# The fp8 product and the eight-head attention of a gated block, joined into one unrolled pipeline by batch

## The reference, cut to what matters

```python
def fake_quant_fp8(t):
    amax = jnp.max(jnp.abs(t))
    scale = FP8_E4M3_MAX / jnp.maximum(amax, 1e-12)
    q = (t * scale).astype(jnp.float8_e4m3fn).astype(jnp.float32)
    return q / scale
# L2_ffn
xq, wq = fake_quant_fp8(x), fake_quant_fp8(weight)
return jnp.einsum('bsd,od->bso', xq, wq) + bias
# L3_xattn: HEADS = 8, DIM_HEAD = 64, SCALE = 64 ** -0.5
q = (x @ Wq).reshape(B, Nq, HEADS, DIM_HEAD)
k = (context @ Wk).reshape(B, context.shape[1], HEADS, DIM_HEAD)
v = (context @ Wv).reshape(B, context.shape[1], HEADS, DIM_HEAD)
sim = jnp.einsum('bihd,bjhd->bhij', q, k) * SCALE
attn = jax.nn.softmax(sim, axis=-1)
out = jnp.einsum('bhij,bjhd->bihd', attn, v)
out = out.reshape(B, Nq, HEADS * DIM_HEAD)
return out @ Wo + bo
# how they are joined
x = x + jnp.tanh(g_ffn[2]) * L2_ffn(layernorm(x))
x = x + jnp.tanh(g_xattn[3]) * L3_xattn(layernorm(x), ctx)
```

## Time and profile before

| | before |
|---|---|
| median of 3 runs | 1619.43 us |
| profiled execution: its time, its span | 1622.06 us, 1620.3 us |
| busy share of the span | PE 75%, DVE 63%, ACT 42%, POOL 34% |
| `fp8_product`, first to last DVE instruction | 993.6 to 1028.8 us |
| `stage_attention8`: start, first scores, last addition to x | 1029.1, 1053.3, 1330.0 us |
| `stage_moe`, first instruction | 1330.7 us |

### The profile page before, as it was taken

One profiled execution on the slowest core, in us unless ns is written; L12 is line 12 of the kernel. 1 busy time (PEld: TensorE's weight loads), 2 busy tenths in 40 slices (PEclk: granted clock), 3 DMA queues, 4 the chain that ended last, 5 costly groups with the idle time before them and its releaser, 6 DMA issues. The chain is left out here.

```text
span 1620.3 us, 31081 instructions
## 1 busy us (share of the span) xinstructions
PE 1211.6 (75%) x10597; PEld 822.1 (51%) x10597; DVE 1017.7 (63%) x3901; ACT 688.1 (42%) x1990; POOL 548.5 (34%) x758
## 2 busy tenths in 40 slices
PE   2277664666677678965989882578888879999997
PEld 2154222343344446643777771255556556777765
DVE  6346759999991498633677776664645554534442
ACT  2133335665664344311445441164646453433342
POOL 5978876887864365313232310000000000000000
PEclk9569875757667799975999996689999898898988
DMA  6400040000003211000000000000000000000001
GB/s 150 126 2 2 1 116 8 20 24 17 28 20 108 71 37 34 14 14 7 2 3 3 3 3 0 11 1 10 0 10 10 1 1 1 1 0 0 0 0 52
DMA packets 64560, 36.94 MB, mean 23 GB/s; under 512 B 24053, under 2 KB 61553, under 8 KB 64435
## 3 DMA queue, kind: packets, MB, share of 16 engines
q1 hardware_dynamic: 63130, 35.02, 7.9%
q10 hardware_dynamic: 1304, 0.33, 0.1%
HBM read 25.21 MB, written 6.42 MB: 20 GB/s over the span
## 5 line engine op out<-in xcount | busy, mean ns | idle before, releaser
L2693 DVE SCALAR_TENSOR_TENSOR k_X<-ps,m_gt,k_X 128x128 f32 (+1 forms) x256 | 72.1, 344 | 126.0 <-PE ps L2592 126.0
L2622 ACT ACTIVATE m_hid<-ps,k_b 128x512 f32<-128x512 f32 x128 | 81.8, 684 | 138.1 <-PE ps L2592 127.7
L2592 PEld LDWEIGHTS ps<-k_w,m_hid 128*128 128x128 f32 x1024 | 123.1, 192 | 26.8 <-issue 17.2
L2583 PE MATMUL ps<-m_xnT,k_w 128*128 128x512 f32 x256 | 131.1, 644 | 1.1 <-DVE m_lg L2638 1.1
L2592 PE MATMUL ps<-k_w,m_hid 128*128 128x128 f32 x1024 | 123.4, 275 | 0.0
L2476 ACT ACTIVATE l_p<-ps,l_shift 128x128 f32<-128x128 f32 x256 | 89.9, 377 | 73.9 <-DVE l_shift L2521 73.9
L2114 DVE TENSOR_REDUCE g_top<-ps 128x8 f32<-128x1024 f32 x64 | 75.4, 1219 | 50.7 <-PE ps L1982 50.7
L121 POOL TENSOR_TENSOR m_rstd<-m_ve,k_half 128x8 f32<-128x8 f32 x4 | 6.5, 1636 | 286.3 <-DVE m_ve L114 286.3
L1379 DVE MATCH_REPLACE8 c_left<-c_top,c_left 128x128 f32<-128x128 f32 x384 | 100.9, 275 | 0.0
L2062 ACT ACTIVATE g_pT<-ps 128x1024 f32<-128x1024 f32 x64 | 62.1, 1022 | 84.9 <-PE ps L1998 84.9
L121 POOL TENSOR_TENSOR l_rstd<-l_ve,k_half 128x8 f32<-128x8 f32 x4 | 6.5, 1636 | 234.6 <-DVE l_ve L114 234.6
(11 more groups left out here) (523 smaller groups left out, 3275.7 us busy)
## 6 DMA issues: line engine op xcount, KB each, us to landing
v_toep<-kpad SPq DMA_DIRECT2D x4, 1024.0 KB, 10.6
fo_dram<-c_fo SPq DMA_DIRECT2D x32, 128.0 KB, 1.7
v_late<-kpad SPq DMA_DIRECT2D x4, 1024.0 KB, 10.5
d_fo<-fo_dram SPq DMA_DIRECT2D x8, 512.0 KB, 3.6
k_X<-in_x SPq DMA_DIRECT2D x8, 256.0 KB, 3.6
out<-k_X SPq DMA_DIRECT2D x4, 512.0 KB, 5.3
f_cx<-in_ctx SPq DMA_DIRECT2D x4, 384.0 KB, 4.9
c_cx<-in_ctx SPq DMA_DIRECT2D x4, 384.0 KB, 3.5
```

Of the source, the lines that this page charges most:

```text
L2583: pe.matmul(ps[:, 4 * u + q, :], k.w1_3[:, e, 128 * q:128 * q + 128], xnT[:, u], start=True, stop=True).then_inc(s["hid_ps"].sem, 1)
L2592: m = pe.matmul(ps[:, 4 * u + 2 + e % 2, j * S:j * S + S], hid[:, u, q, j * S:j * S + S], k.w2_3[:, e, q, :], start=q == 0, stop=q == 1)
L2622: act.activation(hid[:, u, q, :], ps[:, 4 * u + q, :], ACT.Gelu, bias=k.b1_3[:, 2 * e + q:2 * e + q + 1]).then_inc(s["hid"].sem, 1)
L2693: dve.scalar_tensor_tensor(out=xj[u][j], in0=ps[:, 4 * u + 2 + e % 2, j * S:j * S + S], scalar=gt[:, u, j, e:e + 1], in1=xj[u][j], op0=ALU ...
```

## The change: what it does, and the diff

`fp8_product` and `stage_attention8` become one function, `fp8_attention8`, with one block and no loops: 49 steps, n = -15 to 33, written out on every engine. Step n works at several batches and groups at once:

- scores, maxima, exponentials and values of batch n+1; transposes of the weights, the copies of them and weights times values of batch n; output projection and addition to x of batch n-1.
- `item(n)`: for group (n+5)//4, one quarter (128 of 512 columns of the weight) of the keys' and of the queries' projection. Both go through PSUM bank 6, one after the other.
- once in four steps, `due(n, lead)`: the parts of the fp8 product and of the norm of a group, 15 to 6 steps ahead of the group's first batch: bias added to x on POOL (15), scaling on ACT (14), rounding on DVE (13), transpose (12), product (11), addition to x and statistics (10), power on POOL (9), normalising on DVE (7), transpose, copy and the attention's bias on POOL (6).
- The shares move from DVE (one instruction for eight heads) to POOL (two instructions of four heads).
- The copy of the attention result moves from ACT to DVE, the scaling of x for fp8 from DVE to ACT, both bias additions from DVE to POOL.
- The statistics are closed by `bn_aggr` in place of seven small instructions.
- Keys and values are projected from `k.cT` directly; the DMA to `ct` is gone.
- Exponentials are issued in two halves, with the copies of the transposed weights between them.

The diff, cut to the calls and to one part for each engine:

```diff
-        fp8_product(nc, w, ps, k)
+        fp8_attention8(nc, w, ps, k)
...
-        stages = [stage_front, stage_film, stage_mix, stage_attention16, stage_fp8,
-                  stage_attention8, stage_moe]
+        stages = [stage_front, stage_film, stage_mix, stage_attention16, stage_fp8, stage_moe]
...
-                    sp.dma_start(ct[:, u], k.cT[:, bass.ds(t * 2 * W + u * W, W)]).then_inc(s[f"ct{u}"].sem, 16)
...
+                    pe.wait_ge(q_done, 4 * g + b)
+                    pe.wait_ge(xnT_done, begun(n - 1, 6))
+                    pe.wait_ge(xqT_done, begun(n - 1, 12))
+                    pe.matmul(ps[:, 6, :], k.wk3[:, 128 * b:128 * b + 128], k.cT[:, W * g:W * g + W], start=True,
+                              stop=True).then_inc(k_ps, 1)
+                if 0 <= n - 1 < B:
+
+                    i = n - 1
+                    pe.wait_ge(oT_done, i + 1)
+                    pe.wait_ge(v_done, min(i + 2, B))
+                    pe.wait_ge(x8_done, begun(n - 1, 11))
...
-                        dve.tensor_tensor(p[:, a], p[:, a], total[:, a, :].rearrange("p (h o) -> p h o", o=1)
-                                          .broadcast_to([128, H, 128]), ALU.mult).then_inc(s["share"].sem, 1)
...
-                        act.activation(oT[:].rearrange("p a b -> p (a b)"), ps[:, 6, :],
-                                       ACT.Identity).then_inc(s["oT"].sem, 1)
...
+                if 0 <= n + 1 < B:
+                    i = n + 1
+                    dve.wait_ge(p_done, H * (i + 1))
+                    if i >= 3:
+                        dve.wait_ge(share_done, 2 * (i - 2))
+                    dve.reciprocal(rsum[:, i % 3, :], total[:, i % 3, :]).then_inc(rsum_done, 1)
+                if 0 <= n < B:
+                    dve.wait_ge(av_ps, n + 1)
+                    if n >= 2:
+                        dve.wait_ge(out_ps, n - 1)
+                    dve.tensor_copy(oT[:, n % 2].rearrange("p a b -> p (a b)"), ps[:, 4, :]).then_inc(oT_done, 1)
```

More of the change, by code:

```diff
@@ L2240, in _ @@
             dve.tensor_copy(k.wqT[:], ps[:, 2, 0:64].bitcast(BF16))
[L2243 to L2314, removed]
@@ L2337, in stage_attention8 @@
+        top, shift = tmp("top", [128, 2, H]), tmp("shift", [128, 2, H])
+        total, rsum = tmp("total", [128, 3, H]), tmp("rsum", [128, 3, H])
+        p, pT = tmp("p", [128, 3, H, 128]), tmp("pT", [128, 2, H, 128])
+        oT = tmp("oT", [128, 2, 4, 128])
         bo = tmp("bo", [128, 128])
[L2338 to L2340 removed]
@@ L2341, in stage_attention8 @@
         once = ctx.enter_context(OneTime(nc, "l_"))
-        bo_done = once("bo")
-        block = ctx.enter_context(nc.Block())
-        @block.sync
-        def _(sp):
-            with sp.Fori(0, TURNS) as t:
-                for u in range(2):
-                    s["v_ps"].wait(sp, t, 0)
-                    sp.dma_start(ct[:, u], k.cT[:, bass.ds(t * 2 * W + u * W, W)]).then_inc(s[f"ct{u}"].sem, 16)
+        q8_done, exponent, magic, sum_done, xq_done, xqT_ps, xqT_done, o8_ps, xb8_done, x8_done = (
+            once(n) for n in ("q8_done", "exponent", "magic", "sum_done", "xq_done", "xqT_ps", "xqT_done", "o8_ps",
+                              "xb8_done", "x8_done"))
@@ new lines, in fp8_attention8, with due, begun, item @@
+        block = ctx.enter_context(nc.Block())
+        FIRST, LAST = -15, B + 2
+        def due(n, lead):
+            g = (n + lead) // G
+            return g if (n + lead) % G == 0 and 0 <= g < GROUPS else None
+        def begun(n, lead):
+            return min(max((n + lead) // G + 1, 0), GROUPS)
+        def item(n):
+            g, b = (n + 5) // G, (n + 5) % G
+            return (g, b) if 0 <= g < GROUPS else (None, b)
+        def group(g):
+            return k.X[:, G * g:G * g + G, :]
@@ L2357, in _ @@
         @block.tensor
         def _(pe):
-            def opening(t, part):
-                if part == 0:
-                    s["p"].wait(pe, t, 0)
-                    s["ct0"].wait(pe, t, 16)
-                    for b in range(4):
-                        pe.matmul(ps[:, b, :], k.wk3[:, 128 * b:128 * b + 128], ct[:, 0], start=True,
-                                  stop=True).then_inc(s["k_ps"].sem, 1)
-                else:
-                    s["pT"].wait(pe, t, 0)
-                    for u in range(2):
-                        transpose_tokens(pe, s, t, u, xn, ps[:, 4 + u, :], k.ident[:])
@@ L2450, in _, with weights @@
         @block.scalar
         def _(act):
[L2452 removed]
+            def weights(i, a):
                 for b in range(4):
[L2454 to L2485 removed]
```

369 lines of the change are left out of this document (207 added, 162 removed).

## The result

The changed kernel took 1569.57 us (median of 4 runs, 1564.09 to 1571.86) beside 1620.12 us for the kernel before (4 runs, 1618.54 to 1624.72): ratio 0.9679, 95% interval 0.9645 to 0.9712. Forecast were 1567.4 us and 1550 to 1590. The profiled execution took 1568.18 us, its span is 1566.2, against 1620.3 before.

The account below looks back on a forecast made before the run. DVE bounded the old fp8 product and a chain the attention; PE would bound new plain steps. Steps 224.4, fill 36.5, steps -1 and 0 14, drain 7.5: 282.4 against 336.5 us, gain taken as 52, so 1567.4, range 1550 to 1590.

Parts of the forecast that it names:

- Part 1: Plain pipeline step: PE's work sums to 6.92 us, against ACT 4.6 and DVE 4.1, so PE bounds it.
- Part 2: Chain within a step, scores to weights times values: 6.26 us, fits into 6.92 with 0.66 spare; shares on POOL hidden.
- Part 3: Steps with group work, by n mod 4: 9.2, 7.0, 7.5 and 7.2 us; projection's wait for the product's addition 1.75.
- Part 4: DVE beside POOL: shift held by POOL's bias addition at n mod 4 = 1, 0.6 us added per four steps.
- Rival B: Pipeline steps: every shift held about 1 us by POOL's shares, 26 steps about 0.8 longer, 1588 us; chance 0.25.
- Part 5: Fill and drain: first scores at 1030 at the low clock, steps -1 and 0 take 14 us, drain 7.5.
- The sum: Rewritten stretch: 282.4 us against 336.5, a gain of 54, taken as 52 for small semaphore waits.
- Rival A: Faster: clock rises in the fill, step -1 already fast, wait for the product's addition costs nothing; 1549 us, chance 0.17.
- C: Rival, slower: waits on banks 6 and 7 drop PE's clock to 0.50; 12 cold steps give 1650 us; chance 0.02.
- D: Rival: fp8 work stays exposed on in-order queues, giving the product's 35 us back; 1602 us, chance 0.03.

Follow-up runs that it names:

- shares_dve: The changed kernel with its shares on VectorE (DVE) again, as two multiplies right behind the reciprocal, POOL without them: 1603.2 us.
- bias_late: The changed kernel with POOL's two bias additions of a group waiting until the shift of their step is done: 1563.27 us.
- x8_first: The changed kernel with DVE's addition of the fp8 product to x moved ahead of the maximum of its step: 1561.07 us.
- x8_bias: The changed kernel with the product's addition ahead of the maximum and POOL's bias additions behind the shift, old fill: 1552.63 us.
- combo: The changed kernel with the product's addition ahead of the maximum, POOL's bias additions behind the shift, and the fill through banks 0 to 3: 1539.12 us.
- apart_banks: The changed kernel with the fp8 product as a stage of its own ahead again and the fill through banks 0 to 3: 1555.2 us.
- fill_banks: The changed kernel with group 0's key projections early into banks 0 to 3 and its query projections in one burst there: 1551.67 us.
- the burst: The changed kernel with all four key and query projections of a group in one step, through bank 6: 1674.13 us.

## Why the prediction was right

- Part 1. A plain step was forecast at 6.92 and takes 6.66 (1196.92 to 1203.58, from scores to scores). Two terms were too large: the output projection takes 0.89 from start to start (1198.98 to 1199.87), forecast 1.07, and the transposes behind it 0.87, forecast 1.03. The three 512-column matmuls take 2.79 together, forecast 2.7.
- Part 2. The chain was forecast at 6.26; the steps without projections take 6.28. Shares on POOL take 1.04 each and were hidden: the page has L2312 x64, 65.2 us in all, and PE waits nowhere for them in plain steps. That moving them matters was right (35.9 us), but my picture of the loop before was not. I had read that the next maximum stands behind the shares, while its row says that it waited for PE's scores; with the shares on POOL alone the steady step stays at 6.05. The forecast didn't rest on that, since the new step was summed from PE's instructions.
- The shares' price: two of 1.02 on POOL against two of 0.65 on DVE (shares_dve), 1.6 times. The Trainium skill (GPSIMD Engine Reference, 4.1 Engine selection) has about twice; the trace is milder than the rule. At the measured price the transposes wait for nothing in plain steps; that they wouldn't at the rule's is only the prediction's estimate.
- Part 3. Steps of the four kinds: forecast 7.0, 7.5, 7.8 (with the hold of Part 4) and 9.2 for n mod 4 = 3, 0, 1 and 2; measured from scores to scores, as the prediction walks, 6.66, 7.27, 7.52 and 9.66 (by the maxima 7.13, 6.80, 7.52 and 9.66). Sum 31.5 against 31.1. The wait for the addition was 2.18 for a forecast 1.75: the addition takes 0.74, and the shift ahead of it was held. In n mod 4 = 0 the maximum was to come 0.9 late behind the rounding; it is 0.48 late (1.69 behind its scores at 1105.00, 1.21 at 1150.89), which fits into the spare time.
- Part 4. Right in kind, too small in one place: the shift is held not only in n mod 4 = 1, where it costs 0.53 (7.52 against 6.99 in bias_late) for a forecast 0.6, but also in n mod 4 = 2, by the other bias addition, where it lengthens PE's wait. Rival B's general hold didn't come: once the pipeline runs, the shift takes 0.17 to 0.25 us in the other steps, and 0.42 in n mod 4 = 0 (1076.82, 1107.94, 1139.04, 1170.15). The held shift ends with POOL's instruction (1153.21 + 1.26 = 1154.47, 1153.36 + 1.13 = 1154.49), while the addition, with one operand in PSUM, keeps its 0.74 in the middle of POOL's shares (x8_first: 1114.28, with POOL at work from 1113.88 to 1115.92). That agrees with the Trainium skill (SBUF — State Buffer, SBUF: two separate sides), which has the port pair locked for a whole instruction.
- Part 5. First scores forecast at 1030, measured 1032.64, at a granted clock of 0.50 throughout; a round through bank 6 takes 5.6 where nothing comes between (1007.75 to 1013.34), not 5.0, as a 512-column pair takes 2.08 there and not 1.72. Steps -1 and 0: forecast 14, measured 15.7 (first scores to those of step 1, 1048.37). Drain 7.5 and 7.5.
- The sum: 993.02 to 1276.70 is 283.7 us, forecast 282.4. Misses cancel: against the forecast the fill is 3.1 us longer (39.6 for 36.5) and steps -1 and 0 are 1.7 longer, steps 19 to 30 are 3.1 shorter, and in steps 1 to 18 (141.9 for 142.4) the 2.1 of the first long step are made up by the others. That the sum comes within 1.3 us is in part luck. The split of the gain, forecast as 23 from the fill and 29 from the steps, is 20.1 and 33 by the prediction's own cut at the first scores.
- Rival A's two conditions, a clock that rises in the fill and no wait for the addition, didn't hold; C's clock loss came, but once the pipeline ran in a single step. D was wrong as I had put it (the fp8 work hides), yet nearer than I thought: the work was hidden and cost 22 us in waits and PE time.

## What to carry to other kernels

When a stage is merged into a pipeline that is bound by one engine, look which buffer its result shares with that engine's next instruction, and put the operation that frees it ahead of anything with slack: here one addition of 0.74 us behind maximum and shift cost 9.8 us, 1.7 of it clock, more than the merge brought. A fill that runs one group through a single bank pays every round trip; banks that the steady state hasn't begun to use can take it in a burst. And count an engine's relief by the loop that closes the step: 1.2 us off DVE gave nothing in the old steady step, 0.75 in the new.

## What was not expected of the hardware

A wait of 2 to 3 us on PE had a price beyond itself, in some places. Behind the first one PE's granted clock fell (0.66 over 1061 to 1066, in between at its lower level, 0.50 over 1062 to 1064) and the step took 1.7 more than the later ones of its kind, which had the same wait and kept 1.00. In the drain of three kernels (x8_bias, combo, apart_banks) the clock fell too, 0.51 over 3 us in combo, and the drain took 1.3 to 1.4 us longer with the same instructions; of the others only in shares_dve, whose drain is in another order (0.75 over it, 16.6 us):

```profile
1240.00:1243.00 3.00, 2.79 (x13) 2.79 (x14) 0.51 (x2) 0.00 (x0) 1.71 (x2) 0.51 0.00 0
...
1240.21 2.08 PE L2378 MATMUL ps<-k_wo,l_oT 128*128 128x128 f32 x8 [1.11 <-DVE l_oT L2572]
```

(combo: engines in the stretch, and the projection in it, which takes 1.16 in the changed kernel's drain.) What decides between two waits of the same length stays open. The same instructions can also find the clock at either level, as the fills of combo and fill_banks show, so a difference of 2 to 3 us in a fill or in the first steps isn't by itself the edit's. In the burst the clock was low in every group's long step: 0.51 over 1089 to 1102, and 0.50 over 1141 to 1146, 1182 to 1194 and 1230 to 1246, for instance.
